# Attention on one Trainium2 core: geometric exponents moved to SBUF, exponentials in two passes, PSUM banks regrouped

## The chip, the cores and the metric

The kernel runs on one core of one Trainium2 chip, in one launch. The metric is the device time of that core in microseconds, from the first to the last instruction of the program. The profile shown is of one execution, and the times beside it are those of three others.

## What is computed

The reference is one block of a transformer with adaptive layer norm. Two parts follow each other: causal attention over 2 batches x 8 heads, and a two-layer network with local attention. The change touches the first alone. For each of its 16 batch-heads, with T = 2048 positions and D = 32 channels, cut to what matters:

```
scores = einsum('qd,kd->qk', q, k) * scale            # causal: -inf above the diagonal
attn   = softmax(scores);  out = attn @ v
qp = q[..., :3] . head_dir ;  kp = k[..., :3] . head_dir
geo    = qp[:, None] * kp[None, :]                    # causal too
geo_out = softmax(geo) @ v
out = out + head_scale * (geo_out - out)
```

So each batch-head has two softmaxes over the same keys and values: one of the scores, which come from a matrix product, and one of the geometric term, which is an outer product of two vectors.

## The kernel before

The attention stage works on transposed tiles: keys on the 128 partitions, queries along the row. A batch-head has 4 groups of 512 queries, and group g meets the key tiles 0 to 4g+3, which gives 40 steps (`B_STEPS`). The last four steps of each group lie on the diagonal: they are 512, 384, 256 and 128 columns wide, and the others 512. Two steps make a burst, and there are 20 bursts (`BURSTS`) to a head and 16 heads. All five engines have their own program, written out by hand in a fixed order, and wait for each other by semaphores.

A softmax needs the maximum of a row before its exponentials. These maxima are made one head ahead and half a head offset: 40 items (`A_TILES`) of queries by up to 512 keys, one in each step. TensorE multiplies q by k into a bank of `a_ps` (line 718, with a mask product on the diagonal, line 720), and VectorE reduces it (`reduce_max`, line 829). Three times in a head, VectorE puts the maxima of some tiles together (lines 836 to 838), TensorE transposes them into the next bank of `a_ps` (a "rows" item, line 711), VectorE copies them out (line 825), and they travel over HBM into extra rows of the operand q, so that the score product already has the maximum subtracted. The rows items fall into bursts 0, 8 and 14.

One step i then has these parts:

- TensorE, `scores`: the product into half of a slot of `st_ps` (line 733; line 735 adds the mask on the diagonal). A slot is two banks, and there are two slots.
- VectorE, `exponents`: (kp + bound) * qp for the step, written to the other half of the slot (line 850; line 856 masks the diagonal with a minimum). It runs one burst ahead of its step.
- ScalarE: one exponential over both halves (line 801), into a slot of `probs` in SBUF, of which there are four.
- TensorE, `weigh`: the value product of both halves into `o_ps` (line 749, in full float32, the two kinds in different column groups). It runs one burst behind.

In a burst TensorE's order is: two maxima products, two score products, a rows item where there is one, and the four value products of the burst before. VectorE's order is: two reductions with what hangs on them, then the exponents of the next burst's two steps, and now and then another job (`invert` in burst 11, `piece_low`, line 862, in bursts 17 to 19). ScalarE has also `keep` (line 788, the output of a finished group) and `piece_high` (line 792). GpSimd copies values (line 655), starts the store of the maxima and multiplies the finished head by its shares (lines 670 and 674). SP issues nearly all DMAs.

Slots are freed thus: `scores` and `exponents` of step i wait for `probs_ready` of step i-2, since both write the slot that this exponential reads. The product of maxima item n waits for `a_used` of item n-2. The operands q3, k3, vx and raw exist in three sets: SP loads head b+2 at the start of head b (lines 600 to 604), once all scores of head b-1 are made.

Of the kernel before, what the change touches and what calls it, by code (L numbers as in the profile page):

```python
# [12 lines left out]
ACT = mybir.ActivationFunctionType  # L13
AX = mybir.AxisListType

P = 128
B, T, C = 2, 2048, 256
NT = T // P
# [3 lines left out]
GTOK = GT * P  # L22
# [429 lines left out]
def attention_phase(nc, S, io):  # L452
# [6 lines left out]
    BURSTS = NB // 2  # L459
    ROWS = 3 * D  # L460
    MAXROW, ALLROWS = ROWS, ROWS + 2
    PSLOTS = 4
    HALF, VW = 2 * D, D + 1
    SETS = 3
    THIRDS = [slice(n * PIECE // 3, (n + 1) * PIECE // 3) for n in range(3)]
    HIGH_AFTER, LOW_AFTER = (28, 30, 32), BURSTS - 3

# [19 lines left out]
    with ExitStack() as ctx:  # L487
# [19 lines left out]

        dots = geo[0:BH, :, :]
        top, low = (probs[0:BH, 2 * k:2 * k + 2, :, :].rearrange("h s k t -> h (s k t)") for k in range(2))
        a_ps = ps("a_ps", [P, 2, 512])  # L510
        st_ps = ps("st_ps", [P, 2, 2, 512])
        o_ps = ps("o_ps", [P, 2, 512])
        turned_ps = st_ps[:, 0, 0, 0:NT * BH].rearrange("p (t h) -> p t h", h=BH)
        names = ("setup a_ready a_used parts_ready values_in max_in st_ready geo_ready geo_link probs_ready pv_done o_used max_chain "
                 "inverted shared weighed summed sums_in shares_out shares_in o_out piece_hi piece_lo piece_out cleared dots_in kp_turned kp_kept chain rows_out").split()
        q = {n: sem("t_" + n) for n in names}

# [4 lines left out]
        SETUP, CHAIN = 2 * SETS + 1, 5  # L522
        LOAD, SENT, OUT = 16 * 6, 16 * 3, 16 * NG

        PROBS0, PV0, O0 = 1, PSLOTS - 1, 1

        prime(nc, q | dict(enumerate((*loads, *out_sent, *geo_in))), (("probs_ready", PROBS0), ("pv_done", PV0), ("o_used", O0)))

        def chunk(c):
            return slice(c * GTOK, (c + 1) * GTOK)  # L530
# [1 line left out]
        with nc.Block() as block:  # L532

            @block.sync
            def _(sp):
# [61 lines left out]
                        sp.dma_start(S.pieces[part, ds(k, 1)].rearrange("o p n -> p (o n)"), tile[:, :].bitcast(F32)).then_inc(q["piece_out"], 16)  # L597

                def turn(b, s, k, before, more):
                    if more and not (isinstance(b, int) and b + 2 >= BH):  # L600
                        if before:

                            sp.wait_ge(q["st_ready"], b * NB + START)
                        load(b + 2, (s + 2) % SETS)
                    if before:
                        geo_load(b, NG - 1)
                        send(b - 1, NG - 1, (s - 1) % SETS)
                        sums_load(b - 1)
                        send_parts(b - 1)
                    if more:  # L610
                        geo_load(b + 1, 0)
                    maxima_in(b, 1)
                    send(b, 0, s)
                    maxima_in(b, 2)
                    if before:
                        shares_store(b - 1)
                    if more:
                        geo_load(b + 1, 1)
                    send(b, 1, s)
                    if before:  # L620
# [31 lines left out]
            def _(pool):  # L652
# [28 lines left out]
                def turn(b, s, k, before, more):  # L681
                    maxima_out(b, 1)
                    if more:
                        if before:

                            pool.wait_ge(q["pv_done"], (b - 1) * NB + PV0 + START)
                        values(b + 1, (s + 1) % SETS)
                        fetch_piece(b)
                    maxima_out(b, 2)
                    if before:  # L690
                        normalise(b - 1, (s - 1) % SETS)
                    if more:
                        maxima_out(b + 1, 0)
# [8 lines left out]
            def _(pe):  # L702
                def maxima(a, x):
                    n, s = ORDER[a, x], a % SETS
                    if n >= 2:
                        pe.wait_ge(q["a_used"], n - 1 + START)
                    slot = a_ps[:, n % 2, :]
                    if isinstance(x, tuple):
                        first, tiles = PARTS[x[1]]
                        pe.wait_ge(q["parts_ready"], a * len(PARTS) + x[1] + 1 + START)  # L710
                        pe.transpose(slot[0:2 * tiles, 0:P], max_parts[:, 2 * first:2 * (first + tiles)].bitcast(F32), S.ident[:, :]).then_inc(q["a_ready"], 1)
                        return
                    it, c = A_TILES[x]
                    if x == 0:
                        pe.wait_ge(loads[s], a // SETS * LOAD + LOAD + START)
                    width = min(GTOK, (it + 1) * P - c * GTOK)
                    diag = c == it // GT
                    ins = pe.matmul(slot[:, 0:width], q3[s][0:ROWS, it * P:(it + 1) * P], k3[s][0:ROWS, c * GTOK:c * GTOK + width], start=True, stop=not diag)  # L718
                    if diag:
                        ins = pe.matmul(slot[:, width - P:width], S.ident_bf[:, :], mask_n[:, :], start=False, stop=True)  # L720
                    ins.then_inc(q["a_ready"], 1)

                def scores(b, s, i):
# [3 lines left out]
                        if j == 0 and g * GT == first:  # L727
                            pe.wait_ge(q["max_in"], 16 * (b * len(PARTS) + part + 1) + START)

                    pe.wait_ge(q["probs_ready"], b * NB + i - 1 + PROBS0 + START)  # L730
                    out = st_ps[:, i % 2, 0, :]
                    diag = j >= GT * g
                    ins = pe.matmul(out[:, off:GTOK], k3[s][:, j * P:(j + 1) * P], q3[s][:, g * GTOK + off:(g + 1) * GTOK], start=True, stop=not diag)  # L733
                    if diag:
# [3 lines left out]
                def weigh(b, s, i):  # L738

                    g, j = B_STEPS[i]  # L740
                    pe.wait_ge(q["probs_ready"], b * NB + i + 1 + PROBS0 + START)
                    if i == 0:
                        pe.wait_ge(q["values_in"], b + 1 + START)
# [38 lines left out]
            def _(act):  # L782
# [11 lines left out]
                def turn(b, before, more):  # L794
                    for s, (g, j) in enumerate(B_STEPS):
                        off = max(0, j - GT * g) * P

                        act.wait_ge(q["pv_done"], b * NB + s - PSLOTS + 1 + PV0 + START)
                        act.wait_ge(q["st_ready"], b * NB + s + 1 + START)
                        act.wait_ge(q["geo_ready"], b * NB + s + 1 + START)  # L800
                        act.activation(probs[:, s % PSLOTS, :, off:GTOK], st_ps[:, s % 2, :, off:GTOK], ACT.Exp).then_inc(q["probs_ready"], 1)  # L801
                        if before and s == 2:
                            keep(b - 1, NG - 1)
                        for g0 in range(NG - 1):
# [12 lines left out]
            def _(dve):  # L817
                def maxima(a, x):
                    n = ORDER[a, x]
                    dve.wait_ge(q["a_ready"], n + 1 + START)  # L820
                    if isinstance(x, tuple):
                        part = x[1]
                        if a:
                            dve.wait_ge(max_out, 16 * ((a - 1) * len(PARTS) + part + 1))
                        dve.tensor_copy(max_rows[part][:, :], a_ps[0:2 * PARTS[part][1], n % 2, 0:P]).then_inc(q["a_used"], 1)
                        return
                    it, c = A_TILES[x]
                    width = min(GTOK, (it + 1) * P - c * GTOK)
                    dve.reduce_max(chunk_max[:, it, c:c + 1], a_ps[:, n % 2, 0:width], AX.X).then_inc(q["a_used"], 1)  # L829
                    if x in ENDS:  # L830
                        part = ENDS.index(x)
                        first, tiles = PARTS[part]
# [9 lines left out]
                def exponents(b, i):  # L842
# [2 lines left out]
                    if j == 0:  # L845
                        dve.wait_ge(geo_in[g], 16 * (b + 1) + START)

                    dve.wait_ge(q["probs_ready"], b * NB + i - 1 + PROBS0 + START)
                    out, at = st_ps[:, i % 2, 1, :], slice(g * GTOK + off, (g + 1) * GTOK)
                    ins = dve.scalar_tensor_tensor(out[:, off:GTOK], geo[:, 1, at], kp_t[:, j, ds(b, 1)].rearrange("p o -> p o"),  # L850
                                                   geo[:, 0, at], ALU.add, ALU.mult)
                    if j >= GT * g:
# [1079 lines left out]
```

## Time and profile before

| | |
|---|---|
| median of three runs | 2980.03 us (2976.97 to 2985.27) |
| the profiled execution, its own time | 2979.26 us |
| its span, first to last instruction | 2977.2 us |
| attention stage within the span | 297 to 1323 us, sixteen heads |
| TensorE, VectorE, ScalarE busy in that stage | 945, 909 and 594 of 1026 us |

The time of the profiled execution is 2.1 us more than its span, and 0.8 us below the median of the three. Sums over the trace are made against 2979.26 us. An engine's busy share counts the time in which at least one instruction is in it, and says nothing on whether that time could have been shorter.

### The profile page before, as it was taken

How to read it: one execution, taken by the hardware profiler on the slowest of the kernel's cores; microseconds unless marked ns; L12 is line 12 of the kernel's file. 1: busy time of each engine (PE TensorE's matmuls, PEld its weight loads, DVE VectorE, ACT ScalarE, POOL GpSimd, SP SyncE). 2: the span in 40 equal slices, each digit the busy share in tenths (PEclk: the TensorE clock that was granted, in tenths of full speed). 3: DMA queues.
4: the chain of work that ended last, by engine and by line, in shares of the span. 5: the costliest groups of instructions: out<-in, count | busy, mean ns of one | idle time of the engine just before them, and what ended most of it. 6: DMA issues, size and time to landing. Idle time of an engine off the chain costs nothing. (4 is left out here: it accounts for less than half of the span.)

```text
span 2977.2 us, 44176 instructions
## 1 busy us (share of the span) xinstructions
PE 2580.3 (87%) x14072; PEld 1549.8 (52%) x14072; DVE 2220.6 (75%) x4598; ACT 1502.5 (50%) x2807; POOL 560.2 (19%) x388
## 2 busy tenths in 40 slices
PE   4995999999899999974499999949979999995998
PEld 2442333333333333323377777638856777774777
DVE  4776888989898888957688888725547888883665
ACT  0230555555555555541366666614426666663433
POOL 0110000001010001015333333200003333330000
PEclk7996999999999999987799999979989999998999
DMA  2325343344444344317200000030001000001111
GB/s 84 113 100 151 84 132 102 101 123 107 117 136 120 101 113 113 86 55 248 66 9 9 9 9 9 2 120 17 20 17 48 9 9 9 9 6 36 55 61 39
DMA packets 123897, 204.83 MB, mean 69 GB/s; under 512 B 22560, under 2 KB 71008, under 8 KB 120400
## 3 DMA queue, kind: packets, MB, share of 16 engines
q1 hardware_dynamic: 109040, 163.96, 19.8%
q0 software_dynamic: 8832, 21.80, 2.4%
q10 hardware_dynamic: 5920, 17.75, 1.6%
q8 instruction: 55, 0.90, 0.1%
q14 instruction: 50, 0.41, 0.0%
HBM read 125.30 MB, written 54.26 MB: 60 GB/s over the span
## 5 line engine op out<-in xcount | busy, mean ns | idle before, releaser
L801 ACT ACTIVATE probs<-st_ps 128x1024 f32<-128x1024 f32 (+3 forms) x640 | 550.5, 894 | 468.3 <-PE st_ps L733 192.6
L749 PE MATMUL o_ps<-probs,vx 128*33 128x512 f32 (+3 forms) x2560 | 556.4, 558 | 0.0
L850 DVE SCALAR_TENSOR_TENSOR st_ps<-geo_rows,kp_t 128x512 f32<-128x512 f32 (+3 forms) x640 | 463.2, 742 | 60.9 <-ACT probs L801 58.0
L829 DVE TENSOR_REDUCE chunk_max<-a_ps 128x1 f32<-128x512 f32 (+3 forms) x640 | 361.1, 603 | 44.0 <-PE a_ps L718 24.1
L1224 PE MATMUL local_in_ps<-w_local,local_ht 128*128 128x512 f32 x1152 | 322.7, 417 | 9.8 <-ACT local_sq L1366 5.4
L1385 ACT ACTIVATE local_probs<-local_s_ps,local_bias,local_inv 128x256 f32<-128x256 f32 x512 | 283.0, 564 | 13.9 <-DVE local_bias L1480 13.9
L1660 PE MATMUL ff_ag_ps<-ff_ht_parts,w 128*128 128x512 f32 (+1 forms) x1056 | 259.8, 404 | 33.7 <-DVE ff_gate L1769 25.5
L718 PE MATMUL a_ps<-k,q 96*128 96x512 f32 (+3 forms) x640 | 237.6, 446 | 28.4 <-DVE chunk_max L829 22.2
L749 PEld LDWEIGHTS o_ps<-probs,vx 128*33 128x33 f32 x2560 | 126.7, 114 | 253.2 <-issue 219.8
L1392 ACT ACTIVATE local_pt<-local_pt_ps 128x512 f32<-128x512 f32 x256 | 152.4, 596 | 208.3 <-PE local_pt_ps L1282 200.3
L1476 DVE TENSOR_REDUCE local_top<-local_s_ps 128x4 f32<-128x1024 f32 x128 | 156.8, 1225 | 122.4 <-PE local_s_ps L1268 122.4
L1660 PEld LDWEIGHTS ff_ag_ps<-ff_ht_parts,w 128*128 128x128 f32 (+1 forms) x1056 | 199.9, 192 | 88.8 <-DVE ff_gate L1769 33.9
L718 PEld LDWEIGHTS a_ps<-k,q 96*128 96x128 f32 x640 | 109.9, 199 | 253.8 <-DVE chunk_max L829 138.8
L1224 PEld LDWEIGHTS local_in_ps<-w_local,local_ht 128*128 128x128 f32 x1152 | 207.9, 193 | 58.3 <-issue 18.8
L733 PE MATMUL st_ps<-q,k 98*128 98x512 f32 (+3 forms) x640 | 229.6, 418 | 5.7 <-ACT probs L801 4.2
L1487 DVE TENSOR_SCALAR local_probs<-local_probs,local_rden 128x256 f32<-128x256 f32 x512 | 222.9, 477 | 9.0
L1553 POOL TENSOR_TENSOR local_inv<-local_norm,half 128x16 f32<-128x16 f32 x64 | 186.5, 2915 | 175.0 <-DVE local_norm L1465 107.8
L1673 PE MATMUL ff_y_ps<-ff_w,ff_act_t 128*128 128x256 f32 x1152 | 149.5, 285 | 14.4 <-DVE ff_act_t L1775 13.9
L1292 PE MATMUL local_o_ps<-local_pt,local_v_ring 128*64 128x128 f32 x2048 | 154.6, 282 | 3.3 <-ACT local_pt L1392 3.1
L1282 PE MATMUL local_pt_ps<-ident,local_probs 128*128 128x128 f32 x1024 | 150.7, 280 | 6.3 <-DVE local_probs L1487 1.4
L1673 PEld LDWEIGHTS ff_y_ps<-ff_w,ff_act_t 128*128 128x128 f32 x1152 | 140.5, 190 | 21.2 <-DVE ff_act_t L1775 21.0
L1268 PE MATMUL local_s_ps<-local_k_t,local_q_t 64*128 64x256 f32 x1024 | 146.1, 404 | 0.6 <-ACT local_q_t L1379 0.6
(170 smaller groups left out, 3698.2 us busy)
## 6 DMA issues: line engine op xcount, KB each, us to landing
geo_rows<-geo SPq DMA_DIRECT2D x64, 512.0 KB, 7.5
q<-q_parts SPq DMA_DIRECT2D x48, 256.0 KB, 4.2
k<-k_parts SPq DMA_DIRECT2D x48, 256.0 KB, 6.4
piece_lo<-in_pieces POOLq DMA_DIRECT2D x15, 768.0 KB, 5.5
weight_parts<-piece_hi SPq DMA_DIRECT2D x15, 768.0 KB, 3.3
weight_parts<-piece_lo SPq DMA_DIRECT2D x15, 768.0 KB, 5.9
raw<-out_t SPq DMA_DIRECT2D x128, 64.0 KB
shares_in<-shares SPq DMA_DIRECT2D x64, 128.0 KB, 4.8
```

What stands on the lines that cost most here:

```text
L718: ins = pe.matmul(slot[:, 0:width], q3[s][0:ROWS, it * P:(it + 1) * P], k3[s][0:ROWS, c * GTOK:c * GTOK + width], start=True, stop=not diag)
L733: ins = pe.matmul(out[:, off:GTOK], k3[s][:, j * P:(j + 1) * P], q3[s][:, g * GTOK + off:(g + 1) * GTOK], start=True, stop=not diag)
L749: ins = pe.matmul(o_ps[kind * HALF:kind * HALF + VW, g % 2, off:GTOK], vx[s][:, j, :], probs[:, i % PSLOTS, kind, off:GTOK], start=j == 0, ...
L801: act.activation(probs[:, s % PSLOTS, :, off:GTOK], st_ps[:, s % 2, :, off:GTOK], ACT.Exp).then_inc(q["probs_ready"], 1)
L829: dve.reduce_max(chunk_max[:, it, c:c + 1], a_ps[:, n % 2, 0:width], AX.X).then_inc(q["a_used"], 1)
L850: ins = dve.scalar_tensor_tensor(out[:, off:GTOK], geo[:, 1, at], kp_t[:, j, ds(b, 1)].rearrange("p o -> p o"), geo[:, 0, at], ALU.add, AL ...
L1224: last = pe.matmul(in_ps[:, j, :], ht[:, p, a, k, :], w[:, b, k, j * INNER:(j + 1) * INNER], start=i == 0, stop=i == len(steps) - 1)
L1385: last = act.activation(probs[:, hd, :], s_ps[:, a, x % 2 * 2 * P:(x % 2 + 1) * 2 * P], ACT.Exp, bias=bias[:, hd:hd + 1], scale=inv[:, p, ...
L1487: last = dve.tensor_scalar(probs[:, hd, :], probs[:, hd, :], rden[:, hd:hd + 1], None, ALU.mult)
L1553: pool.tensor_tensor(inv[:, p, :], norm2[:, :], S.half[:, :], ALU.pow).then_inc(q["inv_done"], 1)
L1660: last = pe.matmul(ag_ps[0:rows, x % 2, half, :], w1[:, a, k, c0:c0 + rows], ht_parts[:, b, k, :], start=i == 0, stop=i == len(steps) - 1)
L1673: last = pe.matmul(y_ps[:, t, :], act_t[:, a, x, t * P:(t + 1) * P], w2[:, b, x, :], start=(x, i) == (0, 0), stop=x == HC - 1 and i == len ...
```

## The change

- `geo_x`, a new tensor in SBUF with four slots of 512 columns, takes the geometric exponents. They no longer lie in PSUM.
- The eight PSUM banks are dealt anew: three to `a_ps` (were two), three single ones to `st_ps` (were two slots of two), two to `o_ps` as before.
- ScalarE's exponential of a step becomes two: one from `st_ps` once the scores are there, one from `geo_x` once the exponents are there. The first counts up a new semaphore, `st_used`, the second `probs_ready`.
- `scores` of step i waits for `st_used` of step i-3, `exponents` of step i for `probs_ready` of step i-4, a maxima product for item n-3. `weigh` waits for `st_used` and `probs_ready` of its own step.
- The operand sets go from three to two. SP loads head b+1 at the start of head b, behind the same wait as before. GpSimd's value copy waits until the value products of head b-1 are all done (it was b-2).

```diff
-    PSLOTS = 4
+    PSLOTS, GSLOTS = 4, 4
+    ABANKS, STBANKS = 3, 3
-    SETS = 3
+    SETS = 2
...
+        geo_x = sb("geo_x", [P, GSLOTS, GTOK])
-        a_ps = ps("a_ps", [P, 2, 512])
-        st_ps = ps("st_ps", [P, 2, 2, 512])
+        a_ps = ps("a_ps", [P, ABANKS, 512])
+        st_ps = ps("st_ps", [P, STBANKS, 512])
...
-        PROBS0, PV0, O0 = 1, PSLOTS - 1, 1
+        PROBS0, ST0, PV0, O0 = GSLOTS - 1, STBANKS - 1, PSLOTS - 1, 1
...
-                    if more and not (isinstance(b, int) and b + 2 >= BH):
-                        if before:
-
-                            sp.wait_ge(q["st_ready"], b * NB + START)
-                        load(b + 2, (s + 2) % SETS)
+                    if more and before:
+
+                        sp.wait_ge(q["st_ready"], b * NB + START)
+                        load(b + 1, (s + 1) % SETS)
...
-                            pool.wait_ge(q["pv_done"], (b - 1) * NB + PV0 + START)
+                            pool.wait_ge(q["pv_done"], b * NB + PV0 + START)
...
-                    if n >= 2:
-                        pe.wait_ge(q["a_used"], n - 1 + START)
-                    slot = a_ps[:, n % 2, :]
+                    if n >= ABANKS:
+                        pe.wait_ge(q["a_used"], n - ABANKS + 1 + START)
+                    slot = a_ps[:, n % ABANKS, :]
...
-                    pe.wait_ge(q["probs_ready"], b * NB + i - 1 + PROBS0 + START)
-                    out = st_ps[:, i % 2, 0, :]
+                    pe.wait_ge(q["st_used"], b * NB + i - STBANKS + 1 + ST0 + START)
+                    out = st_ps[:, (b * NB + i) % STBANKS, :]
...
+                    pe.wait_ge(q["st_used"], b * NB + i + 1 + ST0 + START)
                     pe.wait_ge(q["probs_ready"], b * NB + i + 1 + PROBS0 + START)
...
                         act.wait_ge(q["st_ready"], b * NB + s + 1 + START)
+                        act.activation(probs[:, s % PSLOTS, 0, off:GTOK], st_ps[:, (b * NB + s) % STBANKS, off:GTOK], ACT.Exp).then_inc(q["st_used"], 1)
                         act.wait_ge(q["geo_ready"], b * NB + s + 1 + START)
-                        act.activation(probs[:, s % PSLOTS, :, off:GTOK], st_ps[:, s % 2, :, off:GTOK], ACT.Exp).then_inc(q["probs_ready"], 1)
+                        act.activation(probs[:, s % PSLOTS, 1, off:GTOK], geo_x[:, s % GSLOTS, off:GTOK], ACT.Exp).then_inc(q["probs_ready"], 1)
...
-                    dve.wait_ge(q["probs_ready"], b * NB + i - 1 + PROBS0 + START)
-                    out, at = st_ps[:, i % 2, 1, :], slice(g * GTOK + off, (g + 1) * GTOK)
+                    dve.wait_ge(q["probs_ready"], b * NB + i - GSLOTS + 1 + PROBS0 + START)
+                    out, at = geo_x[:, i % GSLOTS, :], slice(g * GTOK + off, (g + 1) * GTOK)
```

## Rows read from the trace of the kernel before

**Rows 1.** Busy time by stretch: PE, PEld, DVE, ACT, POOL, clock, DMA share, GB/s.
```profile
297.00:1323.00 1026.00, 945.25 (x4359) 365.81 (x4360) 908.78 (x1772) 594.04 (x748) 101.81 (x107) 0.96 0.41 107
```

**Rows 2.** Who waited for whom in the attention stage: total us, times, longest.
```profile
PE a_ps L711 <- DVE chunk_max L829: 65.8, 46, 2.6
PE a_ps L718 <- DVE chunk_max L829: 8.9, 14, 1.2
...
DVE st_ps L850 <- ACT probs L801: 58.0, 168, 1.1
DVE chunk_max L829 <- PE a_ps L718: 21.7, 16, 2.0
DVE chunk_max L829 <- PE a_ps L720: 15.9, 29, 0.7
```

**Rows 3.** Groups by shape in the attention stage: count, busy us, mean ns, idle.
```profile
L801 ACT ACTIVATE probs<-st_ps 128x1024 f32<-128x1024 f32 x448 | 448.0, 1023 | 356.2 <-PE st_ps L733 192.6 <-DVE st_ps L856 96.5 <-PE st_ps L735 36.7
...
L850 DVE SCALAR_TENSOR_TENSOR st_ps<-geo_rows,kp_t 128x512 f32<-128x512 f32 x448 | 361.5, 833 | 55.2 <-ACT probs L801 52.3
L829 DVE TENSOR_REDUCE chunk_max<-a_ps 128x1 f32<-128x512 f32 x433 | 284.2, 683 | 23.6 <-PE a_ps L718 21.7
...
L801 ACT ACTIVATE probs<-st_ps 128x512 f32<-128x512 f32 x64 | 38.2, 597 | 112.1 <-PE st_ps L735 111.3 <-DVE st_ps L856 0.8
...
L792 ACT ACTIVATE piece_hi<-piece_lo 128x512 fp32r<-128x512 f32 x45 | 28.0, 622 | 0.0
```

**Rows 4.** Timeline, TensorE in one full-width burst: start, duration, idle before.
```profile
799.91 1.91 PE L749 MATMUL o_ps<-probs,vx 128*33 128x512 f32 x8
...
801.75 0.62 PE L718 MATMUL a_ps<-k,q 96*128 96x512 f32 x2
...
802.89 1.91 PE L749 MATMUL o_ps<-probs,vx 128*33 128x512 f32 x8
```

**Rows 5.** Timeline at the turn of a head, at its rows item.
```profile
880.57 0.27 PE L711 MATMUL a_ps<-ident,max_parts 128*8 128x128 f32 x1 [2.55 <-DVE chunk_max L829]
```

**Rows 6.** Busy time by stretch, just behind that turn.
```profile
883.00:886.00 3.00, 3.00 (x10) 0.77 (x10) 2.33 (x5) 1.14 (x3) 0.00 (x0) 0.60 0.70 201
```

**Rows 7.** Waits from 876 to 902 us, bursts 0 to 7 of a head.
```profile
DVE chunk_max L829 <- PE a_ps L718: 1.0, 1, 1.0
DVE st_ps L850 <- ACT probs L801: 0.9, 4, 0.3
```

**Rows 8.** Waits from 902 to 924 us, bursts 8 to 14 of it.
```profile
DVE st_ps L850 <- ACT probs L801: 1.2, 4, 0.6
DVE chunk_max L829 <- PE a_ps L720: 0.7, 1, 0.7
...
PE a_ps L711 <- DVE chunk_max L829: 1.7, 2, 1.1
```

**Rows 9.** Waits from 924 to 940 us, the rest of that head.
```profile
DVE st_ps L850 <- ACT probs L801: 0.7, 1, 0.7
DVE chunk_max L829 <- PE a_ps L720: 0.4, 1, 0.4
```

**Rows 10.** Timeline, VectorE: two exponents alone, and two beside GpSimd's product.
```profile
902.43 1.42 DVE L850 SCALAR_TENSOR_TENSOR st_ps<-geo_rows,kp_t 128x512 f32<-128x512 f32 x2
...
800.88 3.71 DVE L850 SCALAR_TENSOR_TENSOR st_ps<-geo_rows,kp_t 128x512 f32<-128x512 f32 x2 [0.65 <-ACT probs L801]
```

**Rows 11.** Groups by shape, the same operation elsewhere, with SBUF as its target.
```profile
L1769 DVE SCALAR_TENSOR_TENSOR ff_gate<-ff_ag_ps,b,ff_gate 128x512 f32<-128x512 f32 x80 | 59.9, 750 | 73.1 <-ACT ff_gate L1711 73.1
...
L418 DVE SCALAR_TENSOR_TENSOR rot_c<-qk_ps,cos_t 128x512 f32<-128x512 f32 x32 | 22.0, 689 | 39.3 <-PE qk_ps L343 38.5
```

**Rows 12.** Timeline: the operand load at a head's turn.
```profile
876.14 1.35 SPq L585 DMA_DIRECT2D k<-k_parts  x3
```

**Rows 13.** DMA issues, median us to landing.
```profile
k<-k_parts SPq DMA_DIRECT2D x48, 256.0 KB, 6.4
```

**Rows 14.** Timeline before the first head: setting up one operand set.
```profile
258.28 1.76 DVE L888 MEMSET k<- 2x2048 f32 x1 [0.48 <-issue]
```

More of the change, by code:

```diff
@@ L509, in attention_phase @@
         top, low = (probs[0:BH, 2 * k:2 * k + 2, :, :].rearrange("h s k t -> h (s k t)") for k in range(2))
-        a_ps = ps("a_ps", [P, 2, 512])
-        st_ps = ps("st_ps", [P, 2, 2, 512])
+        geo_x = sb("geo_x", [P, GSLOTS, GTOK])
+        a_ps = ps("a_ps", [P, ABANKS, 512])
+        st_ps = ps("st_ps", [P, STBANKS, 512])
         o_ps = ps("o_ps", [P, 2, 512])
-        turned_ps = st_ps[:, 0, 0, 0:NT * BH].rearrange("p (t h) -> p t h", h=BH)
-        names = ("setup a_ready a_used parts_ready values_in max_in st_ready geo_ready geo_link probs_ready pv_done o_used max_chain "
+        turned_ps = st_ps[:, 0, 0:NT * BH].rearrange("p (t h) -> p t h", h=BH)
+        names = ("setup a_ready a_used parts_ready values_in max_in st_ready st_used geo_ready geo_link probs_ready pv_done o_used max_chain "
                  "inverted shared weighed summed sums_in shares_out shares_in o_out piece_hi piece_lo piece_out cleared dots_in kp_turned kp_kept chain rows_out").split()
@@ L523, in attention_phase @@
         LOAD, SENT, OUT = 16 * 6, 16 * 3, 16 * NG
-        PROBS0, PV0, O0 = 1, PSLOTS - 1, 1
-        prime(nc, q | dict(enumerate((*loads, *out_sent, *geo_in))), (("probs_ready", PROBS0), ("pv_done", PV0), ("o_used", O0)))
+        PROBS0, ST0, PV0, O0 = GSLOTS - 1, STBANKS - 1, PSLOTS - 1, 1
+        prime(nc, q | dict(enumerate((*loads, *out_sent, *geo_in))), (("probs_ready", PROBS0), ("st_used", ST0), ("pv_done", PV0), ("o_used", O0)))
         def chunk(c):
@@ L824, in maxima @@
                             dve.wait_ge(max_out, 16 * ((a - 1) * len(PARTS) + part + 1))
-                        dve.tensor_copy(max_rows[part][:, :], a_ps[0:2 * PARTS[part][1], n % 2, 0:P]).then_inc(q["a_used"], 1)
+                        dve.tensor_copy(max_rows[part][:, :], a_ps[0:2 * PARTS[part][1], n % ABANKS, 0:P]).then_inc(q["a_used"], 1)
                         return
@@ L828, in maxima @@
                     width = min(GTOK, (it + 1) * P - c * GTOK)
-                    dve.reduce_max(chunk_max[:, it, c:c + 1], a_ps[:, n % 2, 0:width], AX.X).then_inc(q["a_used"], 1)
+                    dve.reduce_max(chunk_max[:, it, c:c + 1], a_ps[:, n % ABANKS, 0:width], AX.X).then_inc(q["a_used"], 1)
                     if x in ENDS:
```

## Prediction

> **What bounds the kernel now.** I read the busy time by stretch first. The attention stage takes 1026 of the 2977 us, TensorE is busy for 945 of them, VectorE for 909 and ScalarE for 594 [rows 1]. The reader is to see that two engines are nearly full and neither is full: 81 us of TensorE and 117 us of VectorE are idle, in turns, since each waits for the other. ScalarE has room.
>
> The waits say where. TensorE stands 65.8 us in front of line 711, the transposition of the maxima, 46 times with up to 2.6 us, and 8.9 us in front of line 718 [rows 2]. Both name VectorE's reduction, and line 711 waits not for its data (made a burst earlier) but for its bank: with two banks it needs the reduction of the item just before the last, which VectorE reaches only after the exponents and `piece_low` of the burst before. VectorE in turn stands 58.0 us before its exponents, for the exponential that reads the other half of the slot, and 21.7 and 15.9 us before its reductions, for TensorE [rows 2]. That is 95.6 us, 6.0 a head.
>
> The turn of a head has a second price. Behind the wait of 2.55 us [rows 5] the granted clock is 0.60 for 3 us [rows 6], so part of this stretch ran at 1.2 instead of 2.4 GHz: 0.4 x 3.0 = 1.2 us of work lost.
>
> Then I compared work with work. A burst of full width takes TensorE 2.98 us from value products to value products, without a wait: 1.84 us for four value products and 1.14 us for the two maxima and two score products [rows 4]. VectorE needs for the same burst two exponents, which start 0.67 us apart (two take 1.42 us, one 0.75) [rows 10], and two reductions of 0.68 us each at most [rows 3]: some 2.6 us. So TensorE sets the pace in wide bursts. In the diagonal bursts its products shrink while VectorE gets the minimum of line 856 on top, and at the turn it has `piece_low` three times, so there VectorE sets it. I count bursts 8 to 15, mostly wide and without `piece_low`, as TensorE's, and 16 to 7 of the next head as VectorE's.
>
> **The change, part by part.**
>
> *Four slots of exponents.* VectorE now waits for the exponential of step i-4 instead of i-2, two steps or some 3 us older. Its waits for ScalarE go: in the head that I followed 0.9 us in bursts 0 to 7 [rows 7], 1.2 us in 8 to 14 [rows 8], 0.7 us in the rest [rows 9].
>
> *Three banks for the maxima.* Line 711 now needs the item before the two products in front of it, reduced a burst ago. What is late next is the pair of products behind it: they need the two reductions that line 711 used to wait for, so part of the 2.55 us comes back there. Between line 711 and them lie the value products of two narrow steps, under 1 us. At the turn I therefore expect a wait of 1 to 2 us instead of 2.55, and a clock that mostly doesn't fall. In VectorE's terms: its wait of 1.0 us for TensorE in bursts 0 to 7 [rows 7] is the slow stretch behind the turn, and goes with it.
>
> *The sum for a head.* In VectorE's part of the head the gain is what VectorE waited: 1.0 + 0.9 [rows 7] + 0.7 + 0.4 [rows 9] = 3.0 us, of which I take 2.7, since 0.4 is a wait for a maxima product that other work might not cover. In TensorE's part it is what TensorE waited: 1.7 us, two rows items [rows 8]. Together 4.4 us a head, 70 us for sixteen. The head followed has 4.7 us of VectorE waits against a mean of 6.0, so this is not generous; all 95.6 us is what VectorE's waits could give at most.
>
> *The exponents' target.* VectorE's operation at line 850 writes SBUF instead of PSUM. No row has exactly this form. One that takes a pointer operand as here and writes SBUF lasts 750 ns; one with a constant instead and SBUF as its target 689 [rows 11]. Line 850 has the pointer and lasts 0.75 us undisturbed [rows 10]. I take 0, by the nearer row, and keep 0.06 x 640 = 39 us less as the other end. A loss is not to be seen in either row.
>
> *GpSimd beside it.* Two exponents took 3.71 us instead of 1.42 beside GpSimd's product at one place [rows 10], and the mean at full width is 833 ns against 750 [rows 3]: 37 us in all, there before and after. The minimum of line 856 now has both inputs in SBUF and may be held up too; I bound it by 0.3 us a head, 5 us. The Trainium skill's page "SBUF — State Buffer", section "Who interferes with whom", says that a VectorE instruction with two SBUF inputs contends with a GpSimd one that reads SBUF, and that the later one is blocked. The row of 3.71 us agrees; by this rule the 5 us are real, by the rows alone they are open.
>
> *Two exponentials for one.* 1024 elements take 1023 ns, 512 take 597 from PSUM; a 512-wide instruction of ScalarE that reads SBUF takes 622 [rows 3]. Two passes are at most 1.22 us against 1.02: 0.2 x 640 = 125 us of ScalarE, 719 in all, below both others. In latency: a burst's four passes take 2.44 us, and the next burst's value products start 2.98 us after the scores end [rows 4]. So they hide behind the next products, with 0.5 us to spare, except in the seven bursts of a head with a `keep` or `piece_high` of 0.6 us, where 0.1 us may show: 0.7 us a head, 11 us as the upper end. I take 0, because the second value product starts 0.9 us after the first. The passes themselves no longer wait for the later of two inputs. The Trainium skill, page "VectorE: DVE Perf Modes", section "The TRN2 errata", charges each ScalarE instruction with an SBUF source 224 cycles on top of its elements. By that the added passes cost 0.19 us each, an estimate, and the sum is the same, as ScalarE stays under 720 us.
>
> *Behind ScalarE's new wait.* If the exponents are late, the next step's score pass and `keep` stand behind the wait. TensorE's scores need `st_used` of three steps ago, and exponents are made a burst ahead, so this binds only when VectorE is 3 us behind; it is, at times, at the turn, and then VectorE is the bound anyway.
>
> *More waits on TensorE.* Each `weigh` has one wait more, always fulfilled when the other is. No row prices it. Nothing is the lower end. For the upper: a step's value products take 0.92 us [rows 4], which at 2.4 GHz is 4.3 cycles a column; were the products themselves four whole cycles, 0.853 us, the 0.07 left would hold everything else, a wait included: 0.07 x 640 = 45 us. I take 0, as the array works off what was issued before.
>
> *Two operand sets.* SP's load has its old place and its old wait, and the same six DMAs; what changes is that it is for the next head, not the one after. It is issued at 876 us [rows 12] and needs 6.4 us to land [rows 13]; the next head's first product comes in burst 8, 26 us later. Cover: 18 us; nothing is queued on SP that was not before. GpSimd's value copy waits for products that end within 1 us of its old start; the fetch of a weight piece behind it has ten bursts. Both cost nothing. One set less is prepared before the first head, on VectorE's chain: 1.76 + 0.48 us and a short memset [rows 14], 2.3 us gained.
>
> **Sum.** 2979.3 - 70 - 2.3 = 2907 us; I write 2906, with a little for the first 24 maxima items, which also get a third bank.
>
> **The rivals.**
>
> *VectorE gets cheaper as well.* If the SBUF target is worth 0.06 us, two thirds of the 39 us lie where VectorE sets the pace: 2906 - 26 = 2880. For it: the row of 689 ns. Against it: the row of 750. TensorE's floor is further down. Chance 0.14.
>
> *The turn stays.* If VectorE's backlog moves the whole wait from line 711 to the products behind it, the clock falls as before. What remains is ScalarE's share of VectorE's waits, 0.9 + 0.7 us [rows 7, 9], and half of the 1.7: 2.4 us a head, so 2979.3 - 38 - 2 = 2939. For it: VectorE works without a pause through this wait. Against: the clock fell only after 2.55 us in one piece. Chance 0.18.
>
> *It does nothing.* The two engines are so close to each other that the slack is refilled at other places; within 9 us of before. Against it: waits of 4.7 us a head on a path that alternates. Chance 0.06.
>
> *Slower, by the added waits.* In front of every step's value products stands a second wait, on the engine that sets half of the pace. It decides from 73 / 640 = 0.11 us each; at 0.15 us it takes 96 us and the time is 3002. Against: by [rows 4] there is only 0.07 us for all of it. Chance 0.06.
>
> **The numbers.** My forecast has 0.56, with a range of its own from 2885 to 2930. From 2868 to 2948 I leave out the slower case, half of the case without effect, and the tails: that is the range. A change of 0.3% is about what a measurement of this kernel can tell. Faster by more: 0.56 + 0.14 + 0.18 = 0.88; same 0.06; slower 0.06.
>
> **What would show it.** Line 711's waits should fall from 65.8 us to below 15, some of it coming back at line 718. VectorE's waits for ScalarE's exponentials should be gone, its total waits be under 40 us, and a head last 59.6 instead of 64 us, with a clock nearer to 1.0 behind the turn. Line 850 should last 750 ns, and two passes of ScalarE 1.0 to 1.2 us. The prediction is wrong if line 850 lasts 690 or over 800, if value products start to wait for ScalarE, or if line 718 inherits all of line 711's wait.

## The result, and the profile after

The changed kernel takes 2888.82 us (median of four, 2888.75 to 2896.74) against 2981.31 us of the kernel before (median of four), a ratio of 0.9697 with a 95% interval of 0.9675 to 0.9718. That is 92 us less, where 75 were forecast. The profiled execution is the slowest of the four, 2896.74 us, so sums over the trace are made against that: 82.5 us less than the profiled execution of before.

Busy time by stretch shows that the whole gain is in the attention stage and just before it (columns as in [rows 1]). The stage took 1026 us and takes 950. TensorE is idle for 32 of them instead of 81, and VectorE for 64 instead of 117. What comes behind the stage takes 1654.5 us and took 1653.2.

```profile
290.00:1240.00 950.00, 917.95 (x4361) 359.08 (x4361) 886.22 (x1773) 651.15 (x1389) 105.30 (x107) 0.97 0.44 117
```

The waits of the stage, in the order of [rows 2]. The transposition of the maxima (now line 712) waits 0.9 us instead of 65.8. The maxima products behind it (line 719) wait 27.3 us instead of 8.9, 15 times, which is once at every turn from head to head and 1.8 us each on the mean. VectorE waits 4.0 us for ScalarE instead of 58.0, and 39.1 us for TensorE, about what it was.

```profile
PE a_ps L719 <- DVE chunk_max L832: 27.3, 15, 1.9
PE st_ps L734 <- DMA q<-maxima: 2.0, 3, 1.7
PE a_ps L712 <- DVE max_parts L841: 0.9, 5, 0.2
...
DVE chunk_max L832 <- PE a_ps L719: 34.8, 68, 0.9
DVE chunk_max L832 <- PE a_ps L721: 4.3, 13, 0.5
DVE geo_x L853 <- ACT probs L804: 4.0, 7, 1.3
```

The groups by shape answer to [rows 3]. The exponents (line 853) last 807 ns on the mean instead of 833, the two passes of ScalarE 595 and 628 ns, and the minimum on the diagonal 342 on the mean, where it was 299.

```profile
L853 DVE SCALAR_TENSOR_TENSOR geo_x<-geo_rows,kp_t 128x512 f32<-128x512 f32 x448 | 346.3, 807 | 4.0 <-ACT probs L804 4.0
L832 DVE TENSOR_REDUCE chunk_max<-a_ps 128x1 f32<-128x512 f32 x433 | 284.1, 683 | 36.8 <-PE a_ps L719 34.8
L804 ACT ACTIVATE probs<-geo_x 128x512 f32<-128x512 f32 x448 | 281.4, 628 | 6.2 <-DVE geo_x L859 6.2
L802 ACT ACTIVATE probs<-st_ps 128x512 f32<-128x512 f32 x448 | 266.8, 595 | 227.6 <-PE st_ps L734 133.3 <-PE st_ps L736 94.0
...
L859 DVE TENSOR_TENSOR geo_x<-geo_x,later 128x128 f32<-128x128 f32 x256 | 87.5, 342 | 8.8
```

The view of the tile `geo_x` has minimum, median and maximum of both VectorE operations. The medians are 740 ns for the exponents and 292 ns for the minimum; the same view of before has 752 and 299.

```profile
L853 DVE SCALAR_TENSOR_TENSOR geo_x<-geo_rows,kp_t x640: 337/740/2519, 290.1 to 1234.6; 128x512 f32<-128x512 f32 x160
...
L859 DVE TENSOR_TENSOR geo_x<-geo_x,later x256: 291/292/1154, 290.8 to 1235.0; 128x128 f32<-128x128 f32 x128
```

The minimum was never longer than 300 ns before. Now it lasts over 1.1 us fifteen times, once at each turn, and beside each of these GpSimd copies the values (line 656). Before, that copy fell fifteen times on the narrowest exponents, which then took 943 ns instead of 350. So the narrow exponents became shorter by as much as the minimum became longer. Before, then after:

```profile
881.94 0.94 DVE L850 SCALAR_TENSOR_TENSOR st_ps<-geo_rows,kp_t 128x128 f32<-128x128 f32 x1
L850 DVE SCALAR_TENSOR_TENSOR st_ps<-geo_rows,kp_t 128x128 f32<-128x128 f32 x64 | 31.3, 489 | 0.0
...
831.87 1.14 DVE L859 TENSOR_TENSOR geo_x<-geo_x,later 128x128 f32<-128x128 f32 x1
832.23 0.62 POOL L656 COPY vx<-values 128x512 f32<-128x512 f32 x1
L853 DVE SCALAR_TENSOR_TENSOR geo_x<-geo_rows,kp_t 128x128 f32<-128x128 f32 x64 | 22.0, 344 | 0.0
```

A turn of a head in the timeline, to be laid beside [rows 5]. The transposition starts 0.23 us behind the last mask and waits for nothing, its four narrow value products follow, and then TensorE stands 1.92 us. The VectorE lines show why: the reduction that frees the bank starts at 829.97, behind two exponents, two minima and a subtraction on a weight piece.

```profile
827.52 0.23 PE L736 MATMUL st_ps<-mask_t,ident_bf 128*128 128x128 bf16 x1
...
827.75 0.27 PE L712 MATMUL a_ps<-ident,max_parts 128*8 128x128 f32 x1
827.95 0.84 PE L751 MATMUL o_ps<-probs,vx 128*33 128x256 f32 x8
...
829.37 0.68 DVE L865 TENSOR_TENSOR piece_lo<-piece_lo,piece_hi 128x512 fp32r<-128x512 f32 x1
...
829.97 1.28 DVE L832 TENSOR_REDUCE chunk_max<-a_ps 128x1 f32<-128x512 f32 x2
830.71 0.92 PE L719 MATMUL a_ps<-k,q 96*128 96x512 f32 x2 [1.92 <-DVE chunk_max L832]
...
832.08 1.70 PE L751 MATMUL o_ps<-probs,vx 128*33 128x512 f32 x8
```

Another turn of the same execution has nearly the same wait, but here the granted clock is at the lower of its two levels, 1.2 GHz, behind it, and the same eight records of value products last 3.20 us instead of 1.70.

```profile
949.66 1.07 PE L719 MATMUL a_ps<-k,q 96*128 96x512 f32 x2 [1.84 <-DVE chunk_max L832]
...
951.59 3.20 PE L751 MATMUL o_ps<-probs,vx 128*33 128x512 f32 x8
```

The mean granted clock of the two heads is 1.00 and 0.94. Over the sixteen heads it lies between these two. It fell at 11 of the 15 turns, where it had fallen at 14 of 15 before with their waits of 2.55 us. In the whole stage TensorE had the lower level for 58.8 us, and for 90.5 us before. Half of the difference, 16 us, is an estimate of the work that this gave back.

```profile
822.00:881.00 59.00, 56.74 (x277) 22.16 (x275) 56.16 (x113) 40.82 (x88) 6.67 (x7) 1.00 0.48 127
940.00:999.00 59.00, 57.16 (x271) 22.91 (x271) 54.62 (x110) 39.31 (x85) 6.25 (x7) 0.94 0.49 123
```

Before the first head, VectorE has one operand set less to prepare (line 891, formerly three of these), and its first exponents come at 290.06 us instead of 296.56. Its first reduction comes at 275.31 us and came at 277.47.

```profile
256.12 1.76 DVE L891 MEMSET k<- 2x2048 f32 x1 [0.48 <-issue]
...
275.31 1.09 DVE L832 TENSOR_REDUCE chunk_max<-a_ps 128x1 f32<-128x128 f32 x3
...
290.06 0.75 DVE L853 SCALAR_TENSOR_TENSOR geo_x<-geo_rows,kp_t 128x512 f32<-128x512 f32 x1
```

### The profile page after: what moved, and what is told of

It reads as the page before. It is cut to its first block and busy times, and to the rows that moved or that the text cites. A ratio compares the mean times of both kernels' runs of the same rounds, so it can differ in the third digit from the quotient of the medians.

```text
span 2894.7 us, 45406 instructions
## 1 busy us (share of the span) xinstructions
PE 2549.8 (88%) x14072; PEld 1542.4 (53%) x14072; DVE 2194.7 (76%) x4596; ACT 1558.3 (54%) x3447; POOL 563.3 (19%) x388
## 3 DMA queue, kind: packets, MB, share of 16 engines
q1 hardware_dynamic: 109040, 163.96, 20.3%
## 5 line engine op out<-in xcount | busy, mean ns | idle before, releaser
L751 PE MATMUL o_ps<-probs,vx 128*33 128x512 f32 (+3 forms) x2560 | 545.4, 548 | 0.0
L802 ACT ACTIVATE probs<-st_ps 128x512 f32<-128x512 f32 (+3 forms) x640 | 339.2, 530 | 314.3 <-PE st_ps L736 180.7
L853 DVE SCALAR_TENSOR_TENSOR geo_x<-geo_rows,kp_t 128x512 f32<-128x512 f32 (+3 forms) x640 | 437.7, 708 | 4.0 <-ACT probs L804 4.0
L804 ACT ACTIVATE probs<-geo_x 128x512 f32<-128x512 f32 (+3 forms) x640 | 360.9, 564 | 12.9 <-DVE geo_x L859 12.9
L1556 POOL TENSOR_TENSOR local_inv<-local_norm,half 128x16 f32<-128x16 f32 x64 | 186.4, 2912 | 174.9 <-DVE local_norm L1468 107.6
L734 PE MATMUL st_ps<-q,k 98*128 98x512 f32 (+3 forms) x640 | 217.8, 412 | 2.0 <-DMA q<-maxima 2.0
```

Source lines behind the costliest of these rows:

```text
L751: ins = pe.matmul(o_ps[kind * HALF:kind * HALF + VW, g % 2, off:GTOK], vx[s][:, j, :], probs[:, i % PSLOTS, kind, off:GTOK], start=j == 0, ...
L802: act.activation(probs[:, s % PSLOTS, 0, off:GTOK], st_ps[:, (b * NB + s) % STBANKS, off:GTOK], ACT.Exp).then_inc(q["st_used"], 1)
L804: act.activation(probs[:, s % PSLOTS, 1, off:GTOK], geo_x[:, s % GSLOTS, off:GTOK], ACT.Exp).then_inc(q["probs_ready"], 1)
```

## Experiments

All edits are on the changed kernel unless said otherwise. Each time is a median of four runs (ten for the kernel before with two sets); the kernel before ran beside them at 2977.8 to 2980.5 us.

### One part undone at a time

**Two banks for the maxima.**

```diff
-    ABANKS, STBANKS = 3, 3
+    ABANKS, STBANKS = 2, 3
```

> The changed kernel with two banks for the maxima instead of three (seven banks in use). My theory: the rows item again stands for the reduction of the item just before, so the wait in front of the transposition comes back at 50 us or more, with a slower clock behind the turn, while VectorE's waits for exponentials stay near zero. 2.5 to 3 us a head, 2930 to 2937 us. Rival, VectorE's backlog alone decides at the turn and the bank only moves the wait: 2889 to 2897 us, with the wait of the transposition back and that of the maxima products gone by as much.

Measured: 2922.19 us, ratio to the kernel before 0.9808 (0.9788 to 0.9828). The waits of its stage:

```profile
PE a_ps L712 <- DVE chunk_max L832: 53.2, 45, 2.6
PE st_ps L734 <- DMA q<-maxima: 1.0, 1, 1.0
PE a_ps L719 <- DVE chunk_max L832: 0.6, 3, 0.2
```

The rows item stands as it did before, up to 2.6 us, and the products behind it stand no more: the wait has moved back. The sum differs by 26 us (53.8 against 28.2 for these two lines), and so do the profiled executions (2923.23 against 2896.74). The medians differ by 33 us, 2.1 a head. So the third bank is worth somewhat less than the 2.5 to 3 us expected, which put the time 8 us too high at the least, and much more than the rival's nothing. The slower clock of my theory did not come: the lower level lasts 55 us in the stage, against 59. From the first reduction to the first exponents it is 19.1 us again, as in the kernel before.

**Two banks for the scores.**

```diff
-    ABANKS, STBANKS = 3, 3
+    ABANKS, STBANKS = 3, 2
```

> The changed kernel with two banks for the scores instead of three. My theory: with two passes the score pass of two steps ago is over long before the scores need its bank, so this third bank gives nothing: 2885 to 2894 us. Rival, it is this bank that keeps TensorE from waiting for ScalarE: 2905 us or more, with a wait of the score products for the score pass.

Measured: a median of 2909.78 us, of 2911.68, 2911.34, 2888.48 and 2908.22 us, ratio 0.9742 (0.9703 to 0.9781). One run is where my theory put it, three are some 20 us over. The profile (2911.68 us) shows no wait of the rival's kind that would pay for it: 0.3 us for the score pass, and the rest as in the changed kernel.

```profile
PE a_ps L719 <- DVE chunk_max L832: 27.6, 15, 1.9
PE st_ps L734 <- DMA q<-maxima: 2.7, 2, 1.4
PE a_ps L712 <- DVE max_parts L841: 1.3, 7, 0.2
PE st_ps L734 <- ACT probs L802: 0.3, 1, 0.3
```

What differs is the granted clock, 0.95 against 0.97 over the same window (here the stage goes on to 1257 us).

```profile
290.00:1240.00 950.00, 916.62 (x4287) 363.93 (x4289) 880.86 (x1760) 639.19 (x1362) 97.80 (x105) 0.95 0.45 116
```

The clock falls at 14 of 15 turns instead of 11, and stays down longer: 90.4 us in the stage instead of 58.8. Half of the difference is 16 us of work, by this estimate, and the two profiled executions are 15 us apart (2911.68 and 2896.74). The four runs bear it out: the one at 2888.48 us has a mean clock of 0.946 over the whole program, the three others 0.937 to 0.938. So the third score bank takes no wait away that the trace shows, and the gap goes with the clock. Why it fell more in three runs of four, and whether the missing bank has a part in it, is not shown; the wait in front of it is 1.8 us in either kernel.

**Two slots of exponents.**

```diff
-    PSLOTS, GSLOTS = 4, 4
+    PSLOTS, GSLOTS = 4, 2
```

> The changed kernel with two slots of exponents in SBUF instead of four, so exponents wait for the exponential of two steps ago as before. My theory: VectorE's waits for ScalarE come back at some 60 us, and the time is 2925 to 2945 us. Rival, the third bank of the maxima did it all: the waits come back, but in time VectorE has to spare, and it is 2889 to 2897 us.

Measured: 2912.28 us, ratio 0.9778 (0.9759 to 0.9798).

```profile
DVE geo_x L853 <- ACT probs L804: 46.5, 134, 0.8
...
DVE chunk_max L832 <- PE a_ps L719: 6.4, 8, 0.9
```

Both theories have a part. The wait for ScalarE comes back at 46.5 us, but VectorE's wait for TensorE shrinks from 39.1 to 6.4 us, as it arrives at its reductions later. The four slots are worth 23 us, about half of the wait that they take away, and the time lies between the two ranges.

**The kernel before, with two operand sets.** The `SETS`, `load` and `pv_done` lines of the change alone.

```diff
-    SETS = 3
+    SETS = 2
...
-                        load(b + 2, (s + 2) % SETS)
+                        load(b + 1, (s + 1) % SETS)
```

> The kernel before with nothing changed but the operand sets, two instead of three, with the load for the next head and the later wait of GpSimd. My theory: 2.3 us less, from the set that isn't prepared, 2975 to 2980 us. Rival, operands or values come late: a wait of the first maxima product in burst 8 for the load, 2985 us or more.

Measured: 2975.78 us, ratio 0.9985 (0.9976 to 0.9995), some 4 us less (1.5 to 7) and no wait for operands. Its first exponents come at 294.08 us, 2.5 us earlier than in the kernel before. The converse, three sets in the changed kernel, was not run.

### The price of a wait on TensorE

```diff
                     pe.wait_ge(q["st_used"], b * NB + i + 1 + ST0 + START)
+                    pe.wait_ge(q["geo_ready"], b * NB + i + 1 + START)
+                    pe.wait_ge(q["st_used"], b * NB + i + 1 + ST0 + START)
```

> The changed kernel with two more waits in front of each step's value products, both fulfilled whenever the present ones are. The rival theory of the slower side, a price for each wait: at its upper end of 0.07 us this adds 90 us, 2980 us. My theory, waits on TensorE's queue cost nothing since the array works off what was issued: 2885 to 2900 us.

Measured: 2895.06 us, ratio 0.9711 (0.9694 to 0.9728). The other way, the added wait taken out:

```diff
-                    pe.wait_ge(q["st_used"], b * NB + i + 1 + ST0 + START)
```

> The changed kernel without the added wait for the score pass in front of the value products (the wait for the second pass stays). By my theory nothing: 2885 to 2897 us. If a wait costs 0.02 us or more, 2875 us or less.

Measured: 2892.13 us, ratio 0.9710 (0.9694 to 0.9726). The first has two waits more than the changed kernel in front of each of 640 steps, the second one less. So between the two lie three waits a step, 1920 in all, and 3 us, with some 7 us of uncertainty: under 2 ns each, 5 at most. At the 0.07 us of the upper end it would have been 134 us. The rival of the slower side is out.

### What is left at the turn

**VectorE's weight pieces out of the turn, first attempt.**

```diff
-    HIGH_AFTER, LOW_AFTER = (28, 30, 32), BURSTS - 3
+    HIGH_AFTER, LOW_AFTER = (12, 14, 16), 8
...
-                        if more and p >= LOW_AFTER:
+                        if more and LOW_AFTER <= p < LOW_AFTER + 3:
```

> The changed kernel with VectorE's three subtractions on the weight pieces (0.6 us each) moved from bursts 17 to 19 to bursts 8 to 10, and ScalarE's copies before them from steps 28 to 32 to steps 12 to 16. My theory: VectorE sets the pace at the turn, so up to 1.8 us a head go there, while in bursts 8 to 10 TensorE sets it and they are hidden: 2862 to 2872 us, the wait of some 1.9 us in front of the maxima products at the turn nearly gone. Rival, VectorE is the bound all through and only its sum counts: 2886 to 2895 us.

Measured: 2923.24 us, 34 us slower than the changed kernel, and 51 over the range of my theory. The turn did get better (line 719 waits 7.9 us instead of 27.3), but the waits show two things that I had not looked at. ScalarE's copy at step 12 stands for the piece to land, 32 us in all with its exponentials queued behind it, and TensorE's value products stand for them:

```profile
PE o_ps L751 <- ACT probs L804: 23.3, 10, 3.5
PE st_ps L734 <- DMA q<-maxima: 16.6, 13, 2.3
PE a_ps L719 <- DVE chunk_max L832: 7.9, 12, 1.2
...
ACT piece_hi L794 <- DMA piece_lo<-in_pieces: 32.0, 14, 3.8
```

**Second attempt, two bursts later.** `HIGH_AFTER, LOW_AFTER = (16, 18, 20), 10`.

> The changed kernel with VectorE's three subtractions on the weight pieces moved from bursts 17 to 19 to bursts 10 to 12, and ScalarE's copies from steps 28 to 32 to steps 16 to 20. The earlier attempt put them at steps 12 to 16, and there ScalarE waited up to 3.8 us for the piece to land. My theory: with the landing out of the way the turn loses 1.2 to 1.8 us of VectorE work: 2862 to 2878 us. Rival, the store and load of the maxima for the next head then becomes late (13 waits of the first score product for it in the earlier attempt, 16.6 us): 2880 to 2892 us.

Measured: 2887.7 us, ratio 0.9690 (0.9674 to 0.9706), no different from the changed kernel. The rival holds, at a place that it did not name:

```profile
PE st_ps L734 <- DMA q<-maxima: 14.6, 15, 2.5
PE a_ps L719 <- DVE chunk_max L832: 12.0, 14, 0.9
```

The turn's wait fell from 27.3 to 12.0 us, and 14.6 us came up in front of a score product. The timeline puts it in burst 6, where the third group of a head starts and needs the second part of its own maxima. They went out in burst 0; SP's queue and the landing are the reason that they are late:

```profile
776.71 0.35 SPq L561 DMA_DIRECT2D sums_in<-sums  x1
777.11 0.43 SPq L599 DMA_DIRECT2D weight_parts<-piece_hi  x1
777.59 0.43 SPq L599 DMA_DIRECT2D weight_parts<-piece_lo  x1
778.06 0.92 SPq L555 DMA_DIRECT2D geo_rows<-geo  x1
779.02 1.17 SPq L593 DMA_DIRECT2D q<-maxima  x1
...
785.61 0.73 PE L734 MATMUL st_ps<-q,k 98*128 98x512 f32 x2 [0.35 <-DMA q<-maxima]
```

The load of 4 KB is issued at 779.02 behind three transfers of 2 MB together, and the product that needs it starts 6.6 us later.

**The inversion of the sums earlier too.** The run above, and `if before and p == 8` instead of 11.

> As the run before, and VectorE's inversion of the sums is in burst 8 instead of 11, so that the shares come back earlier, SP waits less for them and sends the maxima of the next head's first part earlier. My theory: the wait of the first score product for the maxima goes, and the time is 8 to 16 us under that of the run before, 2855 to 2868 us. Rival, the maxima come late for another reason (their own trip over HBM) and the time is that of the run before within 5 us.

Measured: 2933.8 us, ratio 0.9851 (0.9835 to 0.9868), 46 us slower than the run above. A miss on both theories. GpSimd's products, which started 4.8 us behind the rows item of burst 14 in the run above, now start 2.7 us ahead of it, where VectorE puts the maxima together: one step of 0.17 us takes 1.20, two exponents 2.43, and the rows item waits for them.

```profile
705.82 2.37 POOL L671 TENSOR_TENSOR raw<-raw,shares_in 128x1024 f32<-128x1024 f32 x1 [13.62 <-DMA shares_in<-shares]
...
707.01 1.20 DVE L840 TENSOR_SCALAR max_parts<-row_max 128x8 fp32r<-128x8 f32 x1
...
708.33 2.43 DVE L853 SCALAR_TENSOR_TENSOR geo_x<-geo_rows,kp_t 128x512 f32<-128x512 f32 x2
708.56 0.27 PE L712 MATMUL a_ps<-ident,max_parts 128*16 128x128 f32 x1 [0.51 <-DVE max_parts L841]
```

That and the wait in burst 6, which has grown to 27.8 us over the stage, go in the right direction. The two traces account for the rest: TensorE is idle for 55 us of the stage instead of 29, and has the lower clock for 79 us instead of 25, which is 27 us of work by half of the difference. Together that is 53 us, for a stage that is 49 us longer. What share the moved inversion has through GpSimd's products alone is not shown.

**The maxima ahead of the large transfers.** The second attempt, and on SP:

```diff
                         sums_load(b - 1)
-                        send_parts(b - 1)
-                    if more:
-                        geo_load(b + 1, 0)
                     maxima_in(b, 1)
+                    if before:
+                        send_parts(b - 1)
+                    if more:
+                        geo_load(b + 1, 0)
```

> The run with the weight pieces in bursts 10 to 12, and on SP the load of the maxima of a head's second part moved ahead of the store of the weight pieces and of one load of geometric rows, so that it isn't queued behind 2 MB. My theory: the wait of the score products in burst 6 (14.6 us in 15 places, one a head, with a slower clock behind it) goes, 1.1 to 1.8 us a head: 2860 to 2873 us. Rival, the maxima's own trip is as long without them: 2885 to 2890 us.

Measured: 2865.64 us, ratio 0.9620 (0.9604 to 0.9636). The wait is gone (1.7 us, in one place), and 22 us with it: 13 are the wait itself, and the mean clock of the stage is 0.99 instead of 0.98. In the run before it had fallen three times, each time at such a wait (2.54, 1.88 and 1.29 us), for 17 us together. Here it falls at no turn and at no wait in burst 6. Half of the 17, 9 us, is about the rest.

**A fourth bank for the maxima,** on top of that: `ABANKS, STBANKS = 4, 2`.

> As the run before, with four banks for the maxima and two for the scores. My theory: 12 us of waits in front of the maxima products were left at the turn, and the fourth bank takes most of them and the clock's fall with them: 5 to 15 us under the run before, 2850 to 2865 us. Rival: the fourth bank does nothing, as it did alone, and the time is that of the run before within 4 us.

Measured: 2858.3 us, ratio 0.9595 (0.9579 to 0.9611), the best of all: 31 us under the changed kernel and 7 under the run before. The number lies in the range of my theory, but not by its mechanism: the wait in front of the maxima products went from 12.1 to 9.3 us only, and no fall of the clock at a turn was left to be taken away. Of the 6.5 us between the two traces, 1.3 come before the first exponents, and VectorE's wait for the maxima products falls from 8.1 to 2.6 us. The same fourth bank alone:

> The changed kernel with four banks for the maxima and two for the scores. Two banks for the scores cost nothing of their own (the runs with two showed 2888 to 2912 us, their trace differing from the changed kernel's in the clock at the turns alone). My theory: what is left at the turn is that the second product of the pair needs its bank, and a fourth bank lets TensorE run one more item ahead, so the wait of 1.9 us in front of the maxima products falls to about 1 us and the clock falls less often: 2865 to 2885 us. Rival, VectorE's backlog alone decides and TensorE waits at the next place: 2887 to 2912 us.

Measured: 2893.15 us, ratio 0.9703 (0.9687 to 0.9719), no gain. The wait at the turn was 21.0 instead of 27.3 us, and the score product's wait for the maxima 9.4 instead of 2.0. Alone, the bank's gain went into that second wait, which is 3.3 us with the weight pieces and the maxima moved. Which of the two moves lets the gain stay was not tested.

## Why the prediction was right

**The sum for a head.** Forecast 4.4 us. From the first exponents to the last copy of the output the stage was 1026.8 us and is 949.6, 77.2 less, 4.8 a head. A head is 59.4 us against 59.6 forecast. By the starts of the score products in the timelines, on the mean of the second to the fifteenth head:

| us | bursts 0 to 7 | 8 to 14 | 15 to 19 | head |
|---|---|---|---|---|
| before | 26.2 | 22.6 | 15.9 | 64.7 |
| the changed kernel | 24.6 | 20.2 | 15.0 | 59.8 |
| it, with two banks for the maxima | 24.9 | 21.5 | 15.0 | 61.4 |
| it, with two slots of exponents | 25.0 | 20.3 | 15.7 | 61.0 |

The forecast had 1.9, 1.7 and 1.1 for the three parts (less 0.3 for a wait that might stay), and they gave 1.6, 2.4 and 0.9. So the way of counting held: VectorE's waits in its part of the head, TensorE's in the other. What was mis-sized lies in bursts 8 to 14. TensorE's waits there, 1.7 us a head, are gone as counted. But its busy time there fell as well, from 20.8 to 20.2 us, with the clock at the upper level in both kernels. The sum had no term for this, and no run separates its cause. Two readings in the sum were off by a little: the VectorE waits of [rows 7] to [rows 9] are 4.9 us, not 4.7, and 3.0 less 0.4 is 2.6, not 2.7.

**Four slots.** The waits for ScalarE fell from 58.0 to 4.0 us. Undoing this part alone costs 23 us, so half of the wait was slack already, as the 37.6 us in [rows 2] that VectorE then waits for TensorE suggest.

**Three banks.** Line 711's wait was to fall below 15 us and come back in part at the products behind it, as 1 to 2 us a turn. It fell to 0.9 and came back as 1.8 us, 15 times. Undoing it costs 33 us. The clock was to mostly stay up. This step failed: with a wait of 1.8 us it still fell at 11 of 15 turns (14 before), to a mean of 0.94 in some heads and 1.00 in others. In the sum it was 1.0 us a head, VectorE's wait of [rows 7] for the slow stretch. On the mean of the fourteen heads VectorE waited 1.3 us for TensorE in bursts 0 to 7 and still waits 0.6, which is why this part gave less than forecast. The lower level lasted 32 us less in the whole stage.

**The SBUF target.** I took 0 against an end of 0.06 us. The median is 740 ns and was 752, so the target gives 0.01 us. That the pointer operand makes line 850 slower than the 689 ns of [rows 11] is likely by these rows, and no run tested it. The mean at full width is 807 ns; taken against the bound of 800 that was to show the prediction wrong, that is over it. But the bound was set for an undisturbed instruction, and the mean, 833 before, has GpSimd's share in it. GpSimd beside them costs the exponents 67 ns on the mean, 30 us in all at full width (37 by the same reckoning before). The minimum, now with both inputs in SBUF, went from 299 to 342 ns on the mean with a longest of 1154. That is 11 us in all, where I had bounded it by 5. But the narrow exponents, on which GpSimd's copy fell before, take 9 us less, so on the whole nothing was lost. The Trainium skill's page "SBUF — State Buffer", section "Who interferes with whom", names the contention for two SBUF inputs, and the trace agrees: not once over 300 ns with an input in PSUM, fifteen times over 1.1 us with both in SBUF.

**Two exponentials.** 595 and 628 ns were forecast as 597 and 622. ScalarE is busy for 651 us, under the bound of 719, since back-to-back passes overlap, and value products don't wait for it. The Trainium skill, page "VectorE: DVE Perf Modes", section "The TRN2 errata", has 224 cycles for an SBUF source and 172 for PSUM, by its clock of 1.2 GHz an estimate of 43 ns more; here it is 33.

**The added waits.** Taken as 0, measured as under 2 ns each, with 5 as the upper end.

**Two sets and the start.** 2.3 us for the set was forecast; VectorE's first reduction is 2.16 us earlier, and the first exponents 2.5 us in the kernel before with two sets. The first 24 maxima items were named and left at almost nothing. They are the mis-sized term: from the first reduction to the first exponents it was 19.1 us (277.47 to 296.56) and is 14.75 us (275.31 to 290.06). The run with two banks has 19.1 us again, so the 4.3 us are the third bank's.

VectorE's waits for ScalarE and TensorE together were to be under 40 us and are 43.1 (95.6 before), a small miss.

**From 75 to 92.** In the traces 82.5 us: 77.2 in the stage instead of 70, 6.5 before it instead of 2.3, and the rest of the program 1.2 longer. The other three runs are 8 us faster than the profiled one. Their mean clocks are 0.943 to 0.945 against 0.942, which goes the right way, but they have no trace, and it is not shown that this is all. By the medians the result is near the lower end of the forecast's own range, 2885; that it isn't under it is in part luck, since no term of the sum holds the shorter products of bursts 8 to 14 or the 4.3 us of the start. Undone one by one, the parts make 33 + 23 + 4 = 60 of the 92 us, or 81 with the 21 us between the medians of the score bank's run, which go with the clock. The rest is shared between them, or belongs to the exponential that no longer waits for the later of two inputs; the kernel with both parts undone was not run, nor one with a single exponential.

## What to carry to other kernels

Where two engines set the pace in turns, add what the one that sets it waits for, part by part; a wait in the part where the other rules is slack, and taking it away gives half or nothing. Behind every wait that is removed there is a next one with a date, here a load of 4 KB behind 2 MB in the same queue: before work is moved, look at when its input lands and at what gets nearer to it. A fourth bank that gave nothing alone gave 7 us once that load and the weight pieces had been moved, so parts should be tried again after the bound has moved.

## What the runs showed of the hardware

- The TensorE clock fell, or not, at a wait of nearly the same length at the same place of the program: 1.70 us against 3.20 us for the same eight records, behind 1.92 and 1.84 us of waiting. It fell at 11 of the 15 turns of the changed kernel, at 14 of 15 with waits of 2.55 us before, and at none in the run with the maxima moved ahead, where they were 1.0 us at most. Four runs of one kernel (two banks for the scores) spread over 23 us, 2888.48 at a mean clock of 0.946 and 2908 to 2912 at 0.937 to 0.938.
- A fulfilled semaphore wait in TensorE's queue costs nothing that can be measured (3 us over 1920 of them, with 7 us of uncertainty).
- VectorE's small operations last longer beside GpSimd as well: 1.20 us instead of 0.17 for one on 8 columns beside its product, 1154 ns instead of 292 for the minimum beside its copy of 0.62 us.
